# Two layer norms of an adaLN block: the wide passes go from GpSimd to ScalarE

## What is computed

```python
mod = (silu(c) @ wmod)                      # 6 vectors per row: sa, ca, ga, sb, cb, gb
h = layernorm(x) * (1 + ca) + sa            # norm 0
x = x + ga * attn(h)                        # mLSTM with RMS norm, gates, output projection
h = layernorm(x) * (1 + cb) + sb            # norm 1
x = x + gb * ffn(h)                         # router, top 2 of 8 experts, relu MLP
# layernorm(x) = (x - mean) / sqrt(var + 1e-5), over the 128 features of a token
```

## Time and profile before

| | us |
|---|---|
| median of 3 runs (350.1 to 371.14) | 351.06 |
| the profiled execution | 350.73 |
| its span, first to last instruction | 348.9 |
| TensorE busy | 324.0 (93%) |
| VectorE busy | 277.1 (79%) |
| GpSimd busy | 176.4 (51%) |
| ScalarE busy | 164.6 (47%) |

### The profile page before, as it was taken

One profiled execution on the slowest core, in us unless ns is written; L12 is line 12 of the kernel. 1 busy time (PEld: TensorE's weight loads), 2 busy tenths in 40 slices (PEclk: granted clock), 3 DMA queues, 4 the chain that ended last, 5 costly groups with the idle time before them and its releaser, 6 DMA issues.

```text
span 348.9 us, 4964 instructions
## 1 busy us (share of the span) xinstructions
PE 324.0 (93%) x1704; PEld 260.0 (75%) x1704; DVE 277.1 (79%) x794; ACT 164.6 (47%) x300; POOL 176.4 (51%) x177
## 2 busy tenths in 40 slices
PE   2999869899999999999999999999999999878995
PEld 1978756688778877878687868786878688666883
DVE  5576774589969996999789987999679968784774
ACT  1442423246455545465536544564646363334442
POOL 7720640237834884288526864486407832584340
PEclk9999995689999999999999999999999999998999
DMA  4770000600043002500160006100610042004201
GB/s 127 233 195 0 2 0 3 240 3 1 0 151 123 3 0 83 191 0 1 25 250 2 0 3 243 30 0 0 241 36 0 0 186 88 1 1 178 96 0 30
DMA packets 13726, 24.13 MB, mean 69 GB/s; under 512 B 1779, under 2 KB 8102, under 8 KB 12678
## 3 DMA queue, kind: packets, MB, share of 16 engines
q1 hardware_dynamic: 13474, 23.70, 19.9%
q10 hardware_dynamic: 164, 0.07, 0.1%
q0 software_dynamic: 64, 0.07, 0.1%
HBM read 21.60 MB, written 2.23 MB: 68 GB/s over the span
## 4 chain that ended last, share of the span: by engine, by line
PE 77%; DVE 7%; POOL 5%; DMA 4%; ACT 2%; issue 2%; SPq 1%; DVEq 0%; POOLq 0%
PE bank L1008 10%; PE bank L1017 8%; PE bank L1027 8%; PE bank L1009 8%; PE bank L1010 8%; PE bank L1018 8%; PE bank L975 5%; PE bank L960 3%; PE bank L908 2%; DMA gate_bc<-gates_d 2%; DMA br_bc<-in_L_ffn_br_dram 2%; PE bank L1048 2%; PE bank L1034 2%; PE bank L1042 2%; PE bank L923 1%
## 5 line engine op out<-in xcount | busy, mean ns | idle before, releaser
L447 POOL TENSOR_TENSOR hg_lo<-hg,hg_hi 128x512 fp32r<-128x512 f32 x69 | 92.6, 1354 | 77.7 <-ACT hg_hi L501 77.7
L804 DVE SCALAR_TENSOR_TENSOR hg<-bank,neg_b,gate_bc 128x512 f32<-128x512 f32 x128 | 94.6, 743 | 33.4 <-DMA gate_bc<-gates_d 18.1
L501 ACT ACTIVATE hg_hi<-hg 128x512 fp32r<-128x512 f32 x128 | 79.9, 630 | 79.6 <-DVE hg L804 78.5
L1008 PE MATMUL bank<-h_hi,w_hi 128*128 128x512 f32 x128 | 59.3, 464 | 2.3 <-ACT gate_rows L539 2.3
L1009 PE MATMUL bank<-h_hi,w_lo 128*128 128x512 f32 x128 | 51.5, 403 | 0.0
L1010 PE MATMUL bank<-h_lo,w_hi 128*128 128x512 f32 x128 | 51.4, 401 | 0.0
L1017 PE MATMUL bank<-hg_hi,w_hi 128*128 128x512 f32 x128 | 51.3, 401 | 0.0
L1027 PE MATMUL bank<-hg_lo,w_hi 128*128 128x512 f32 x128 | 51.0, 399 | 0.0
L1018 PE MATMUL bank<-hg_hi,w_lo 128*128 128x512 f32 x128 | 50.6, 395 | 0.0
L816 DVE TENSOR_TENSOR hg_lo<-hg,hg_hi 128x512 fp32r<-128x512 f32 x59 | 43.2, 732 | 0.5
L416 POOL TENSOR_SCALAR var_eps<-mv 128x4 f32<-128x4 f32 x16 | 4.9, 306 | 74.6 <-DVE mv L573 74.6
(11 more groups left out here) (160 smaller groups left out, 554.9 us busy)
## 6 DMA issues: line engine op xcount, KB each, us to landing
gate_bc<-gates_d SPq DMA_DIRECT2D x8, 1024.0 KB, 6.9
gate_bc<-gates_d SPq DMA_DIRECT2D x16, 256.0 KB, 3.5
gate_bc<-gates_d SPq DMA_DIRECT2D x8, 512.0 KB, 4.9
out_dram<-x_all SPq DMA_DIRECT2D x8, 256.0 KB, 2.3
w_raw<-in_L_ffn_W_dram SPq DMA_DIRECT2D x1, 1024.0 KB, 9.0
x_all<-in_L_attn_x_dram SPq DMA_DIRECT2D x2, 256.0 KB, 4.1
wmod_sb<-in_L_wmod_dram SPq DMA_DIRECT2D x1, 384.0 KB, 4.8
gates_d<-gate_rows SPq DMA_DIRECT2D x8, 16.0 KB
```

What stands on the lines that cost most here:

```text
L447: g.tensor_tensor(hg_lo[k][:, :], hg[k][:, :], hg_hi[k][:, :].bitcast(fp32), ALU.subtract).then_inc(s_lo_pool, 1)
L501: a.activation(hg_hi[k][:, :], hg[k][:, :], ACT.Copy).then_inc(s_hghi, 1)
L804: v.scalar_tensor_tensor(hg[k][:, :], up_bank[n % 4][:, :], neg_b1[:, n:n + 1], gate_bc[own % 2][:, n // NU, :], ALU.max, ALU.mult).then_i ...
L1008: t_.matmul(dst, w_hi, hx, start=True, stop=False)
```

## The change

`norm` on GpSimd keeps only four-wide work: `var_eps`, `minus_mean`, `rstd`, and `shift` = -mean * `rstd`. ScalarE has a new `norm_apply`: four instructions, one for each tile of 128 tokens, that compute `xn` = x * `rstd` + `shift` with scale and bias read per token. It stands on ScalarE's queue at t = 8 for norm 1, behind `hg_hi` of that step and ahead of `h_ga`; at t = 13 for norm 0 of row b+3; and for the first row ahead of the opening turns. The wait for the transposes that read the buffer before goes to ScalarE; on GpSimd a wait for the previous `norm_apply` of the same norm takes its place.

```diff
-            def norm(k, b, first=False):
+            def norm(k, b):
                 wait_apart(pool, s_mv[k], b + 1)
+                if b:
+                    pool.wait_ge(s_xn[k], b)
                 g.tensor_scalar(var_eps[k][:, :], mv[k][:, :, 1], LN_EPS, None, ALU.add).then_inc(s_ve[k], 1)
-                if k == 0 and not first:
-                    wait_apart(pool, s_xT, b)
-                g.tensor_tensor(xn[k][:, :, :], row(x_all, b).rearrange("p (j d) -> p j d", j=NT),
-                                bcast(mv[k][:, :, 0], D), ALU.subtract).then_inc(s_xc[k], 1)
+                g.tensor_scalar(minus_mean[k][:, :], mv[k][:, :, 0], -1.0, None, ALU.mult).then_inc(s_mm[k], 1)
                 pool.wait_ge(s_ve[k], b + 1)
                 g.tensor_tensor(rstd[k][:, :], var_eps[k][:, :], minus_half[:, :], ALU.pow).then_inc(s_rs[k], 1)
-                pool.wait_ge(s_xc[k], b + 1)
+                pool.wait_ge(s_mm[k], b + 1)
                 wait_apart(pool, s_rs[k], b + 1)
-                g.tensor_tensor(xn[k][:, :, :], xn[k][:, :, :], bcast(rstd[k][:, :], D), ALU.mult).then_inc(s_xn[k], 1)
+                g.tensor_tensor(shift[k][:, :], minus_mean[k][:, :], rstd[k][:, :], ALU.mult).then_inc(s_sh[k], 1)
...
+            def norm_apply(k, b):
+                act.wait_ge(s_sh[k], b + 1)
+                if k == 0 and b:
+                    act.wait_ge(s_xT, b)
+                for j in range(NT):
+                    last = a.activation(xn[k][:, j, :], x_all[:, b * T + j * P:b * T + (j + 1) * P], ACT.Identity,
+                                        bias=shift[k][:, j:j + 1], scale=rstd[k][:, j:j + 1])
+                last.then_inc(s_xn[k], 1)
+
+            norm_apply(0, 0)
             act.wait_ge(s_mods, 1)
...
+                    if t == 8 and end:
+                        norm_apply(1, m1)
+                    if t == 13 and ahead:
+                        norm_apply(0, b + 3)
                     if t == 8 and start:
                         a.activation(h_ga[:, :], hT[:, :], ACT.Copy, scale=mods[:, 2, bass.ds(m2, 1)]).then_inc(s_hga, 1)
```

More of the change, by code:

```diff
@@ L142, in adaln_mlstm_moe_kernel @@
         var_eps = [sb(f"var_eps{k}", [P, NT]) for k in range(2)]
+        minus_mean = [sb(f"minus_mean{k}", [P, NT]) for k in range(2)]
         rstd = [sb(f"rstd{k}", [P, NT]) for k in range(2)]
+        shift = [sb(f"shift{k}", [P, NT]) for k in range(2)]
         xn = [sb(f"xn{k}", [P, NT, D]) for k in range(2)]
@@ L230, in adaln_mlstm_moe_kernel @@
         s_rs = [sem(f"s_rs{k}") for k in range(2)]
-        s_xc = [sem(f"s_xc{k}") for k in range(2)]
+        s_mm = [sem(f"s_mm{k}") for k in range(2)]
+        s_sh = [sem(f"s_sh{k}") for k in range(2)]
         s_xn = [sem(f"s_xn{k}") for k in range(2)]
@@ L447, in body @@
                         g.tensor_tensor(hg_lo[k][:, :], hg[k][:, :], hg_hi[k][:, :].bitcast(fp32), ALU.subtract).then_inc(s_lo_pool, 1)
-            norm(0, 0, first=True)
+            norm(0, 0)
             g.memset(b1_sel[:, :, :], 0.0).then_inc(s_mask0, 1)
```

## The result

The changed kernel takes 352.98 us in the median, the kernel before 349.83 beside it (17 executions each). The ratio is 1.0103, 95% interval 1.0071 to 1.0135: slower by 1%, some 3 us. The prediction was 348.9 with a range of 345.5 to 351.5; so the time lies above the range, and on the other side of no change. The profiled execution takes 355.24 and its span is 353.5, 4.6 above the span of before.

What follows compares the result with a forecast made beforehand. TensorE was taken as the bound, busy 36.22 of 36.60 us per full turn. Gains 0.33 + 1.2 + 0.3 + 0 = 1.8 us off 350.73 gave 348.9; range of all cases 345.5 to 351.5.

Steps and rivals of the forecast that it cites:

- The full turns, priced at 0: Full turns: ScalarE's added 2 x 1.63 us is hidden by TensorE's matmuls, so the gain is 0.
- VectorE gets past GpSimd at the gates: Rival, full turns: `gates` runs ahead of GpSimd's `hg_lo`, saving 6 x 0.38 = 2.3 us, giving 346.6; chance 0.12.
- The second opening turn, 1.2 us: Second opening turn: `rms` begins 1.4 us sooner, `zp` shrinks by 0.86; 1.2 taken between 0.6 and 1.9.
- its lower end: Second opening turn: two weight subtractions fall beside `h_lo`, whose 1.27 us come between, leaving 0.6 of 1.9 us.
- The first opening turn, 0.33: First opening turn: `rms` can begin 0.33 us sooner, covered by VectorE's 0.50 us idle; bounds 0 and 0.5.
- The turn without `start`, 0.3: Turn without `start`: `xn` comes 0.45 us sooner for TensorE's transposes; 0.3 taken, bounds 0 and 0.5.
- The prices: Each norm: four ScalarE activations 1.63 us, one 0.485; GpSimd's queue held 1.8 us, `shift` 0.25, power about 1.0.
- ScalarE's queue as the bound: Rival, full turns: `norm_apply` delays ScalarE's queue; at a step of 1.0 each turn loses 0.6 us, 352.5; chance 0.05.
- The clock: Rival: TensorE's spells at half clock between 52 and 72 us shorten, 345.9, or lengthen, 352.4; chances 0.12 and 0.07.
- the reverse of the clock: The clock rival's slower sign: 7 us more at half clock costs 3.5 us, giving 352.4; chance 0.07.

Runs made afterwards that it cites:

- ScalarE's part alone: The kernel before, with each norm's four activations added on ScalarE into a spare tensor nothing reads: 350.44 us, ratio 1.0012.
- `top_d` late: The changed kernel with `top_d` and the four index searches (`max_index`) moved behind the `m_row` scan: 348.53 us against 350.00, ratio 0.9978.
- the run with the reorder in the kernel before: The kernel before with `top_d` and the four index searches moved behind the `m_row` scan: 355.28 us against 349.58, ratio 1.0195.
- the two late weight subtractions: Second opening turn's last two `w_lo` moved to t = 14 and 15: reordered changed kernel 344.87 and 346.20 us; kernel before 348.32, ratio 0.9917.

## Why the prediction was wrong, point by point

- **The full turns, priced at 0: this step failed.** It measured +0.59 us a turn. The step followed what ScalarE's new work delays, found cover for it, and was right there: ScalarE's part alone lengthens no turn. What it left out is the other half of the change. It put GpSimd's freed time down as a possible gain, at most 0.38 us a turn, and gave it no way to lose. But `rms` was a place where GpSimd held VectorE back; with `rms` sooner, VectorE and all that follows it moved, and a small instruction with two SBUF inputs, `top_d`, fell at the beginning of a pass of GpSimd's and not at its end: 1.12 us where it took 0.25, and TensorE waits 0.66 us a turn for the scan behind it. The prediction had used this contention in the opening, for `zp`, and in a rival, for `gates`; it did not ask which other VectorE instruction would meet GpSimd when VectorE runs sooner.
- **The rival "VectorE gets past GpSimd at the gates"** had the right pair of engines and the wrong instruction, and only one sign. `gates` takes 1056 ns in the mean after and 990 before; it hardly changed, although it begins only 0.08 us behind its `hg_lo` where it was 0.18. Its price was wrong too. With `top_d` late the order does turn and `gates` takes 0.26, but the turns fall by 0.1 us and not by 0.38: the 0.25 us in a turn that TensorE idles ahead of the next experts' matmul for `gate_rows` stay, and they were most of the 0.38.
- **The second opening turn, 1.2 us.** Here the mechanism was right. VectorE's idle time ahead of `rms` squared fell from 1.90 to 0.90 (0.5 forecast), `zp` fell from 1.02 to 0.16 as said, and L959, the old L943, no longer idles (0.77 in the earlier trace rows). Counted from the end of `ms_eps`, `a_col` begins 6.39 us later where it was 7.15, and `gates` 9.23 where it was 10.21: 0.8 to 1.0 gained. The first full turn nevertheless begins only 0.58 sooner, and that sum has the clock in it: `ms_eps` itself comes 2.55 later after, 0.9 of it carried over from the first opening turn and the rest gathered from 38 to 42 us, behind a spell at the low clock from 36 us on; and from `gates` to the first full turn it is 2.15 less, without the spell from 52 to 62. So it is chance that the total lies at the lower end. VectorE's opening after, with GpSimd's power at the head:

```profile
46.63 1.38 POOL L436 TENSOR_TENSOR rms<-ms_eps,minus_half 128x4 f32<-128x4 f32 x1 [0.41 <-DVE ms_eps L766]
...
50.24 1.73 POOL L443 TENSOR_TENSOR h_lo<-h2T,h_hi 128x512 fp32r<-128x512 f32 x1 [2.23 <-ACT h_hi L500]
...
48.05 0.16 DVE L728 TENSOR_TENSOR rms<-rms 128x4 f32<-128x4 f32 x1 [0.90 <-POOL rms L436]
...
49.66 0.16 DVE L782 TENSOR_TENSOR_SCAN zp<-ones,zg 128x3 f32<-128x3 f32 x1
...
50.13 2.38 DVE L678 TENSOR_TENSOR w_lo<-w_raw,w_hi 128x512 fp32r<-128x512 f32 x2
```

  The power takes 1.38 and not 1.0, with VectorE's `w_lo` beside it from 46.47, and the two `w_lo` behind `zp` take 2.38 where they took 1.28, with `h_lo` beside them. That is the case that the text described for its lower end.
- **The first opening turn, 0.33.** It came, and did not show in the time: counted from the end of `ms_eps`, `rms` squared begins 1.18 us later, where it was 1.50. But `ms_eps` itself comes 1.22 later, most of that from a pair of TensorE's matmuls at 14 us, which takes 1.91 where it took 1.02; why, the trace doesn't show.
- **The turn without `start`, 0.3.** It went the other way: TensorE idles 1.85 us for `xn`, where it was 1.66. The power takes 1.54, `shift` 0.28, the four activations 1.65, so the shift is ready only at 304.4 and not 1.8 us after the norm's begin at 301.96. The power took 1.49 in this place before as well; the prediction reckoned 1.0, from the opening.
- **The prices.** Right: 480 ns for one activation with two per-token operands (485 forecast), 1.64 us for four (1.63), 0.20 for `shift` (0.25), and 192.91 - 191.02 = 1.9 us on GpSimd for the norm (1.8).
- **ScalarE's queue as the bound** did not come: a step of 0.39, where 0.38 was forecast. **The clock** moved in kind: the spell from 52 to 62 us is gone, one from 36 to 42 came, and at the end spells at 304 and 320 us stand in place of one from 312 to 320; other traces have such spells at other places, those with the old norm too.
- **The range** ended at 351.5; of the two slower cases, the reverse of the clock (352.4) and ScalarE's queue (352.5), neither was this one, and both were left out of it. A case "a VectorE instruction with two SBUF inputs on the path to TensorE meets a GpSimd pass" could have been priced from the trace of before: one pass of 1.25 us less the 0.25 of `top_d`, less the turn's 0.38 of slack, is 0.62 a turn, in six turns 3.7 us, or 352.6 by the sum.

## What to carry to other kernels

Where two engines exclude one another for whole instructions, taking work off one of them shifts the phase of the other's queue, and that is worth either sign: before pricing the freed time at zero or better, list the small instructions of the other engine that lie on the path of the busiest one, and see which pass each would meet. If such an instruction feeds nothing urgent, it can go behind the one that does; but look first at what waits for it and at which pass the ones behind it then meet, since the same reorder brought 4.6 us in one kernel here and cost 5.7 in the other. And an experiment that holds the freed engine for as long as it was held before tells a cost of phase from a cost of work.

## What the runs showed of the hardware that was not expected

- A VectorE instruction of four numbers per partition takes 0.13 to 0.15 us alone and 1.0 to 1.25 when it meets a GpSimd pass at its beginning; `gate_b`, of 32, takes 0.18 and 1.27. It holds for `TENSOR_TENSOR` with two SBUF inputs, the scan `zp`, and also for instructions with one SBUF input: `top_s`, a `TENSOR_SCALAR` of 128x4 (0.15 us in the full turn of after, 1.01 in the run with the reorder in the kernel before), and a `COPY` of `rms` (0.13 in the kernel before, 1.23 in the run with ScalarE's part alone). `hg`, which reads PSUM, takes 0.71 to 0.75 us in the kernel before and in the changed one, with GpSimd's passes beside it or not.
- The same edit, `top_d` behind the scan, was worth -4.6 us in one kernel and +5.7 in another that differs from it only in who makes the norms; and spare work on ScalarE, free by itself, took 4.8 of those 5.7 us back.
- What stays open: why the two late weight subtractions end the low clock sooner, and whether the norms on ScalarE, with the reorder, are worth anything beyond that move. For the second the two ratios beside the same kernel before differ by 0.1%, with intervals that overlap.
